# Local attention: queries' product and projection between the two score groups, values' product behind the second, input split three tiles ahead in two buffers

## The reference, cut to what matters

```python
h = shift_token(x)                         # right half of the channels moved down one token
q, k, v = split(h @ wqkv, 3)               # 256 -> 3 x 512, 8 heads of 64
q = l2norm(q) * q_scale;  k = l2norm(k) * k_scale
q, k = rotary_xpos(q, k)                   # x * cos + rotate_half(x) * sin, with a scale by position
# per window of 128 queries: keys and values are the window before and its own
sim  = einsum('bhwid,bhwjd->bhwij', q * 8, k)          # 128 x 256 per head
attn = softmax(where(mask, -max, sim))
o    = einsum('bhwij,bhwjd->bhwid', attn, v)
x = x + o @ wo
```

## Time and profile before

| what | value |
|---|---|
| median of 3 runs | 3078.51 us (3073.59 to 3085.33) |
| profiled execution, own time | 3081.87 us, span 3080.3 us, mean granted TensorE clock 0.935 |
| busy over the span | PE 2612.9 us (85%), PE weight loads 1544.9 (50%), DVE 2212.7 (72%), ACT 1491.3 (48%), POOL 542.4 (18%) |
| first layer's local attention | about 1483 to 2023 us |
| second layer's | about 2284 to 2824 us |
| largest groups of it | L1219 products 327.2 us PE (1152 matmuls), L1375 exponentials 284.1 us ACT, L1475 normalise 221.1 us DVE, L1540 powers 186.4 us POOL |
| means of smaller ones | L1459 scaling of the keys 692 ns DVE, L1382 `copy_probs` 595 ns ACT, L1365 `k_t` 612 ns, L1369 `q_t` 599 ns ACT |
| the chain of waits, as far as the page names it | PE 4%, DVE 2%, DMA 1%: it covers the last feed-forward phase only |

### The profile page before, as it was taken

How to read it: one execution, slowest core, us unless ns; L and a number is a source line. 1 busy time by engine, 2 the same in 40 slices (tenths; PEclk the granted TensorE clock), 3 DMA queues, 4 the chain that set the end, 5 groups by cost and what they waited for, 6 DMA issues and landing times. The chain is left out here.

```text
span 3080.3 us, 47691 instructions
## 1 busy us (share of the span) xinstructions
PE 2612.9 (85%) x14040; PEld 1544.9 (50%) x14040; DVE 2212.7 (72%) x4456; ACT 1491.3 (48%) x2777; POOL 542.4 (18%) x356
## 2 busy tenths in 40 slices
PE   4995899898898999884499999949969999995998
PEld 2442333333333333323366666628856666664777
DVE  5777788788887888866677777725547777774565
ACT  0320455555554555561366666624426666664343
POOL 0100000000100000015333333300013333331000
PEclk8996899999998999997799999979989999998999
DMA  2334244334344443416200000030001000000111
GB/s 87 120 108 105 68 127 126 98 97 120 100 113 114 119 115 97 99 60 234 70 9 8 8 9 9 4 111 21 20 15 48 8 7 9 9 7 31 55 57 42
DMA packets 122753, 204.93 MB, mean 67 GB/s; under 512 B 21728, under 2 KB 69920, under 8 KB 119216
## 3 DMA queue, kind: packets, MB, share of 16 engines
q1 hardware_dynamic: 108912, 163.96, 19.0%
q0 software_dynamic: 7808, 21.79, 2.4%
q10 hardware_dynamic: 5920, 17.75, 1.5%
HBM read 125.30 MB, written 54.26 MB: 58 GB/s over the span
## 5 line engine op out<-in xcount | busy, mean ns | idle before, releaser
L801 ACT ACTIVATE probs<-st_ps 128x1024 f32<-128x1024 f32 (+3 forms) x640 | 547.5, 895 | 525.0 <-PE st_ps L733 251.0
L749 PE MATMUL o_ps<-probs,vx 128*33 128x512 f32 (+3 forms) x2560 | 559.2, 560 | 0.0
L850 DVE SCALAR_TENSOR_TENSOR st_ps<-geo_rows,kp_t 128x512 f32<-128x512 f32 (+3 forms) x640 | 448.3, 716 | 77.9 <-ACT probs L801 73.7
L831 DVE TENSOR_REDUCE chunk_max<-a_ps 128x1 f32<-128x512 f32 (+3 forms) x640 | 367.0, 605 | 89.2 <-PE a_ps L721 50.1
L719 PE MATMUL a_ps<-k,q 96*128 96x512 f32 (+3 forms) x640 | 273.0, 476 | 80.9 <-DVE chunk_max L831 64.6
L1219 PE MATMUL local_in_ps<-w_local,local_ht 128*128 128x512 f32 x1152 | 327.2, 421 | 2.1 <-DVE local_ht L1426 2.1
L1375 ACT ACTIVATE local_probs<-local_s_ps,local_bias,local_inv 128x256 f32<-128x256 f32 x512 | 284.1, 571 | 14.2 <-DVE local_bias L1468 14.2
L1647 PE MATMUL ff_ag_ps<-ff_ht_parts,w 128*128 128x512 f32 (+1 forms) x1056 | 259.6, 404 | 32.2 <-DVE ff_gate L1756 24.0
L719 PEld LDWEIGHTS a_ps<-k,q 96*128 96x128 f32 x640 | 123.5, 203 | 278.0 <-issue 154.5
L733 PE MATMUL st_ps<-q,k 98*128 98x512 f32 (+3 forms) x640 | 225.8, 416 | 39.3 <-ACT probs L801 33.0
L1464 DVE TENSOR_REDUCE local_top<-local_s_ps 128x4 f32<-128x1024 f32 x128 | 156.7, 1224 | 135.9 <-PE local_s_ps L1261 135.9
(11 more groups left out here) (171 smaller groups left out, 3681.1 us busy)
## 6 DMA issues: line engine op xcount, KB each, us to landing
geo_rows<-geo SPq DMA_DIRECT2D x64, 512.0 KB, 7.2
q<-q_parts SPq DMA_DIRECT2D x48, 256.0 KB, 4.3
k<-k_parts SPq DMA_DIRECT2D x48, 256.0 KB, 6.3
piece_lo<-in_pieces POOLq DMA_DIRECT2D x15, 768.0 KB, 5.1
weight_parts<-piece_hi SPq DMA_DIRECT2D x15, 768.0 KB, 3.3
weight_parts<-piece_lo SPq DMA_DIRECT2D x15, 768.0 KB, 5.9
raw<-out_t SPq DMA_DIRECT2D x128, 64.0 KB
shares_in<-shares SPq DMA_DIRECT2D x64, 128.0 KB, 4.0
```

What stands on the lines that cost most here:

```text
L749: ins = pe.matmul(o_ps[kind * HALF:kind * HALF + VW, g % 2, off:GTOK], vx[s][:, j, :], probs[:, i % PSLOTS, kind, off:GTOK], start=j == 0, ...
L801: act.activation(probs[:, s % PSLOTS, :, off:GTOK], st_ps[:, s % 2, :, off:GTOK], ACT.Exp).then_inc(q["probs_ready"], 1)
L831: dve.reduce_max(chunk_max[:, it, c:c + 1], a_ps[:, s % 2, 0:n], AX.X).then_inc(q["a_used"], 1)
L850: ins = dve.scalar_tensor_tensor(out[:, off:GTOK], geo[:, 1, at], kp_t[:, j, ds(b, 1)].rearrange("p o -> p o"), geo[:, 0, at], ALU.add, AL ...
```

## The change

`ht` gets a second buffer. The input is transposed and split three tiles ahead instead of two (`make_later_input`), behind `weigh(t, 0)` instead of behind `weigh(t - 1, 3)`. The queries' product of t+2 goes between the two score groups, ahead of the projection; the values' product of t+1 goes behind scores B and the first two transposes of probabilities; the keys' product of t+2 goes behind the transposed queries. The projection writes bank 1 instead of bank 0. The squares wait for both rotations. On ScalarE the copy of the values goes behind the first two pairs of exponentials, the input's copy between the third and the fourth. On VectorE the residual goes behind `normalise(t, 1)`, the queries are rotated ahead of `normalise(t, 2)`, the low input stands between `normalise(t, 2)` and `(t, 3)`, and the keys are rotated last. GpSimd adds the queries ahead of the keys. The prologue and the written-out tiles (four at the end) follow.

```diff
@@ -1154,7 +1154,7 @@
-ht = sb("ht", [P, 2, CC, P], F32R)
+ht = sb("ht", [P, 2, 2, CC, P], F32R)
@@ -1182,13 +1182,13 @@
 def tiles(eng, body):
-    body(0, 0, 2)
-    body(1, 1, 2)
-    with eng.Fori(1, TILES // 2 - 1) as i:
+    body(0, 0, 3)
+    body(1, 1, 3)
+    with eng.Fori(1, TILES // 2 - 2) as i:
...
-            body(2 * i + p, p, 2, first=False)
-    body(LAST - 1, 0, 1)
-    body(LAST, 1, 0)
+            body(2 * i + p, p, 3, first=False)
+    for t in range(LAST - 3, LAST + 1):
+        body(t, t % 2, LAST - t)
@@ -1208,30 +1208,37 @@
     def _(pe):
         def make_input(u, p):
...
-            pe.wait_ge(q["sq_done"], at(u) + START)
...
-        def make_product(j, signal):
+        def make_later_input(u, p, after_output=True):
+            pe.wait_ge(q["sq_done"], at(u) - 1 + START)
+            if after_output:
+                pe.wait_ge(q["y_read"], at(u) - 3 + START)
+            make_input(u, p)
+        def make_product(j, p, signal):
...
-                last = pe.matmul(in_ps[:, j, :], ht[:, a, k, :], w[:, b, k, j * INNER:(j + 1) * INNER], start=i == 0, stop=i == len(steps) - 1)
+                last = pe.matmul(in_ps[:, j, :], ht[:, p, a, k, :], w[:, b, k, j * INNER:(j + 1) * INNER], start=i == 0, stop=i == len(steps) - 1)
...
-        def make_keys(u):
+        def make_keys(u, p, inputs=2):
+            pe.wait_ge(q["ht_low"], at(u) + inputs + START)
+            if inputs == 1:
+                pe.wait_ge(q["y_read"], at(u) - 2 + START)
+            make_product(1, p, q["k_ready"])
+        def make_queries(u, p):
...
-            make_product(1, q["k_ready"])
-        def make_queries(u, after_output=True):
...
-            if after_output:
-                pe.wait_ge(q["y_read"], at(u) - 2 + START)
-            make_product(0, q["q_ready"])
-        def make_values(u):
+            make_product(0, p, q["q_ready"])
+        def make_values(u, p):
...
-            make_product(2, q["v_ready"])
+            make_product(2, p, q["v_ready"])
         def transpose_rows(g, bank, signal):
@@ -1292,7 +1299,7 @@
-                last = pe.matmul(in_ps[:, 0, 0:C], o_t[:, x, :], wo[:, x, :], start=x == 0, stop=x == KIN - 1)
+                last = pe.matmul(in_ps[:, 1, 0:C], o_t[:, x, :], wo[:, x, :], start=x == 0, stop=x == KIN - 1)
...
         def tile(t, p, more, first=True):
@@ -1301,41 +1308,43 @@
             if not begins:
                 weigh(t - 1, 2)
                 weigh(t - 1, 3)
-            if more == 2:
-                make_input(t + 2, p)
+            if more >= 2:
+                make_queries(t + 2, p)
             if not begins:
                 project(t - 1, more)
-            if more:
-                make_values(t + 1)
             scores(t, p, 1)
             transpose_probs(t, 0, more)
             transpose_probs(t, 1, more)
-            if more == 2:
-                make_keys(t + 2)
+            if more:
+                make_values(t + 1, 1 - p)
             weigh(t, 0)
+            if more == 3:
+                make_later_input(t + 3, 1 - p, not begins)
             if more:
                 transpose_keys(t + 1)
-            if more == 2:
-                make_queries(t + 2, not begins)
             weigh(t, 1)
             if more:
                 transpose_queries(t + 1)
+            if more >= 2:
+                make_keys(t + 2, p, more - 1)
             transpose_probs(t, 2, more)
             transpose_probs(t, 3, more)
...
+        pe.wait_ge(q["ht_low"], at(1) + START)
+        make_input(1, 1)
...
-        make_keys(0)
-        make_queries(0, False)
-        make_values(0)
+        make_keys(0, 0)
+        make_queries(0, 0)
+        make_values(0, 0)
...
-        make_input(1, 1)
+        make_later_input(2, 0, False)
+        make_keys(1, 1)
+        make_queries(1, 1)
...
-        make_keys(1)
-        make_queries(1, False)
@@ -1343,15 +1352,16 @@
     @block.scalar
     def _(act):
-        def make_input(u):
+        def make_input(u, p, reused=True):
...
-            act.wait_ge(q["v_ready"], at(u) + START)
-            act.activation(ht[:, 0, :, :].rearrange("p k n -> p (k n)"), in_ps[:, 1, 0:CC * P], ACT.Copy).then_inc(q["ht_done"], 1)
+            if reused:
+                act.wait_ge(q["v_ready"], at(u) - 1 + START)
+            act.activation(ht[:, p, 0, :, :].rearrange("p k n -> p (k n)"), in_ps[:, 1, 0:CC * P], ACT.Copy).then_inc(q["ht_done"], 1)
         def make_squares(u):
...
+            act.wait_ge(q["rot_k"], at(u) + 1 + START)
@@ -1392,14 +1402,15 @@
                 make_squares(t + 1)
             if not begins:
                 copy_output(t - 1)
-                make_values(t, p)
             exponentials(t, p, 0)
             exponentials(t, p, 1)
-            if more == 2:
-                make_input(t + 2)
+            if not begins:
+                make_values(t, p)
             copy_probs(t, 0)
             exponentials(t, p, 2)
             copy_probs(t, 1)
+            if more == 3:
+                make_input(t + 3, 1 - p)
             exponentials(t, p, 3)
             if more:
                 make_keys(t + 1, 1 - p)
@@ -1407,11 +1418,12 @@
-        make_input(0)
+        make_input(0, 0, False)
+        make_input(1, 1, False)
...
-        make_input(1)
+        make_input(2, 0)
@@ -1421,10 +1433,10 @@
     @block.vector
     def _(dve):
-        def make_low_input(u):
+        def make_low_input(u, p):
...
-            dve.tensor_tensor(ht[:, 1, :, :].rearrange("p k n -> p (k n)"), in_ps[:, 1, 0:CC * P],
-                              ht[:, 0, :, :].rearrange("p k n -> p (k n)").bitcast(F32), ALU.subtract).then_inc(q["ht_low"], 1)
+            dve.tensor_tensor(ht[:, p, 1, :, :].rearrange("p k n -> p (k n)"), in_ps[:, 1, 0:CC * P],
+                              ht[:, p, 0, :, :].rearrange("p k n -> p (k n)").bitcast(F32), ALU.subtract).then_inc(q["ht_low"], 1)
         def make_rotated(u, g, ready, free, signal):
@@ -1478,7 +1490,7 @@
         def residual(t):
...
-            dve.tensor_tensor(S.x3[:, here, :], in_ps[:, 0:1, 0:C], S.x2[:, here, :], ALU.add).then_inc(q["y_read"], 1)
+            dve.tensor_tensor(S.x3[:, here, :], in_ps[:, 1:2, 0:C], S.x2[:, here, :], ALU.add).then_inc(q["y_read"], 1)
         def tile(t, p, more, first=True):
@@ -1486,26 +1498,27 @@
             if more:
                 make_norms(t + 1)
             normalise(t, 0)
+            normalise(t, 1)
             if not begins:
                 residual(t - 1)
-            normalise(t, 1)
-            if more == 2:
-                make_low_input(t + 2)
             maxima(t, p, 1)
             if more:
                 make_keys(t + 1, 1 - p)
-            if more == 2:
+            if more >= 2:
+                rotate_queries(t + 2)
+            normalise(t, 2)
+            if more == 3:
+                make_low_input(t + 3, 1 - p)
+            normalise(t, 3)
+            if more >= 2:
                 rotate_keys(t + 2)
-            normalise(t, 2)
-            normalise(t, 3)
-            if more == 2:
-                rotate_queries(t + 2)
...
-        make_low_input(0)
+        make_low_input(0, 0)
+        make_low_input(1, 1)
@@ -1514,9 +1527,9 @@
+        make_low_input(2, 0)
+        rotate_keys(1)
...
-        make_low_input(1)
-        rotate_keys(1)
@@ -1541,8 +1554,8 @@
         def tile(t, p):
             invert(t + 1, 1 - p)
+            add_queries(t + 2)
             add_keys(t + 2)
-            add_queries(t + 2)
         pool.dma_start(mask_even[:, :, :], io["mask_even"].rearrange("m p n -> p m n")).then_inc(S.masks_in, 16)
         pool.dma_start(mask_odd[:, :, :], io["mask_odd"].rearrange("m p n -> p m n")).then_inc(S.masks_in, 16)
```

## The result

The changed kernel takes 3030.07 us (median of 5 runs, 3028.51 to 3031.06) against 3078.51 us for the kernel before (3073.59 to 3085.33): ratio 0.984, 95% interval [0.9827, 0.9854]. The forecast was 3028 in 3014 to 3056. The profiled executions are 3029.94 us (span 3028.3) and 3081.87 us (span 3080.3).

What follows compares the result with a forecast made beforehand. Local attention is bound by PE's work plus two waits for copies. Gains 53.4 and 2.8 less losses 4.1 and 1.6 give 50.5 us, 3031.4 from the profiled 3081.87; 3028 from the runs' median, range 3014 to 3056.

Steps and rivals of the forecast that it cites:

- the stall: Steady tiles: 0.07 us a tile lost to the collision and two thin covers together, bounds 0 and 0.3.
- The two gaps: PE's waits for the copies of o_t and q_t in steady tiles close, gaining 0.92 us in the mean tile.
- The collision: GpSimd's addition of queries meets group 3's two multiplications, which end at 14.3; transposes 3 want them at 14.38.
- Masks B: Masks B come at 5.80 and can start after exponentials A at 5.65: cover 0.15 us, thinnest on the front half.
- The round trip: Input of t+3 from PE through ACT and DVE back to PE: low part 12.2, keys' product 12.34, cover 0.1.
- rival 1: Back-half covers fail together, low input or multiplications late by 0.3 to 0.6 us a tile: 3051 us, chance 0.19.
- Rival 2: No change: new waits take back 0.9 us a tile, with the collision on group 2: 3078 us, chance 0.07.
- Rival 3: Slower: the squares come too late, so the queries' product and all behind it wait: 3102 us, chance 0.08.
- Rival 4: The granted clock falls from 1.00; with shorter waits nothing speaks for it; no price or chance given.
- The start of a layer: Prologue splits two inputs before the first product: +0.8 us a layer, bounds -2 and +3.
- The ends: Last two tiles of a layer: same gaps go, about 0.9, and the values' copy, 0.5: -1.4 us a layer.
- the forecast's own range: Whole kernel, 3018 to 3040 us: stall 0 and gap 0.99 at one end, gap 0.77 at the other; chance 0.66.

Runs made afterwards that it cites:

- after: The kernel with the whole change and no further edit, against the kernel before: 3030.07 us, ratio 0.984.
- the two kernels under Together: Changed kernel with GpSimd's addition of queries behind normalise(t, 3) and next weights issued by SyncE: 3008.04 us; the same with the second input split later: 3003.58 us.

## Why the prediction was right

The mechanism was right in the steady tiles, the terms less so. Start of each step on PE from masks A, predicted and in the tile shown:

| step | predicted | measured |
|---|---|---|
| queries' product | 2.62 | 2.61 |
| projection | 4.19 | 4.12 |
| masks B | 5.80 | 5.85 |
| values' product | 8.25 | 8.28 |
| input | 10.41 | 10.45 |
| transposed keys | 10.85 | 10.72 |
| keys' product | 12.34 | 12.25 |
| transposes 2 | 13.91 | 13.74 |
| next masks A | 15.07, with the stall 15.14 | 15.12 |

- **The total was in part luck.** The steady tiles gained 54.7 us where 49.3 were forecast, 5.4 more; the starts lost 7.35 where 1.6 were forecast, 5.75 more. The two errors cancel. The 3028 against 3030.07 is closer than the terms that it is made of.
- **The two gaps.** They close, as forecast, shown by the waits of after and by the two experiments that open them again. The tile gained 0.92 and 0.96 us where 0.92 - 0.07 = 0.85 was predicted.
- **The collision.** Place and mechanism as predicted, size not: 0.36 us a tile instead of 0.07, outside its bounds (0 to 0.3). The multiplications were on time: in the tile ahead of the one shown (masks A 14.89 us before 1859.10) they start at 12.63 and end at 14.35, predicted 12.6 and 14.3. What failed is "transposes 3 want it at 14.38": PE starts transposes 2 at 13.72 there, and wants the other half 0.43 later, at 14.15. What offset it: I took 0.47 + 0.69 = 1.16 us for the last transposes, the 0.69 from a row that itself begins with a wait of 0.34. With nothing late they take 0.87, 0.29 less. Also the input cost 0.27 instead of 0.44 and the transposed queries 0.41 instead of 0.49, while the transposed keys took 0.53 instead of 0.41. Two errors of 0.3, of opposite sign, made the tile come out nearly right, which is luck too.
- **Masks B.** 1.73 us from the projection to them instead of 1.61, and no wait of theirs beyond single ones. Their cover was about 0.2 instead of 0.15, by what the values' copy cost once it was used up.
- **The round trip.** Cover about 0.3, not 0.1: in the tile ahead of the one shown the low part ends at 11.91 where the prediction had 12.2. That is why rival 1 had less for it than it seemed. Its other half, the multiplications late at transposes 3 by 0.3 to 0.6, did happen, at 0.36. That the time is not rival 1's 3051 is due to the cheaper transposes, and to this being half of it: the keys' product never waits in after.
- **Rival 2** didn't come: the addition starts at 1856.85, behind the transposed queries and beside group 3, not group 2. **Rival 3** didn't either: the squares of this tile start at 1859.90, 0.80 behind masks A, and are done at 1.82 (predicted 1.8), and the queries' product at 2.61 doesn't wait. **Rival 4**: the clock stays 1.00 in the steady tiles; it fell at the start of the layers instead.
- **The start of a layer** is the mis-sized term: +0.8 us predicted, +3.40 and +3.95 measured, beyond the bound of +3. The prediction named the second input and ScalarE's issues but gave the issues no price; it had the products of tile 1 moved ahead as a gain, and they had been what hid the issues. From masks A to B of tile 0, where the queries' product waits for the squares, it took 1.26 and 2.55 us more than before; from masks B to masks A of tile 1, partly at the lower clock (0.74 and 0.84 granted over this stretch, 1.00 before), 2.87 and 1.60 more (11.94 and 10.67 instead of 9.07); up to masks A, 0.73 and 0.20 less.
- **The ends** -1.45 and -1.48 for -1.4. The rest of the difference between the totals, -1.7, lies in code that wasn't changed.
- **Slips in the working.** The keys are scaled at 8.25 + 0.65 + 0.69 = 9.59, not "8.25 + 0.65 = about 9.55"; 9.55 is what the text goes on with, so nothing hangs on it. By its stated terms, from the median of the runs, the forecast's own range comes to about 3020 to 3037, not 3018 to 3040. And the waits were read from PE's rows alone, where the weight load's row of 16.0 us stood too.

What stays open: why the stretch ahead of local attention scatters by up to 14 us between kernels that have the same code there, which moves the totals of the small experiments; why the start of a layer scatters with the issues on ScalarE; and what the new place of the values' product is worth by itself, which no run isolates.

## What to carry to other kernels

Two waits in a row on PE didn't add here. And the distance from start to start beside a wait isn't a step's cost in a full pipe: the second half of the last transposes read 0.69 behind a wait and is 0.44 without (half of 0.87), the input 0.44 ahead of one and 0.27 without, while the projection read 1.61 behind a wait and 1.73 without. Take durations for a sum from rows with no wait in or beside them. A wait listed for a weight load is a place to look, not a price: the 16.0 us listed before were worth nothing, the 9.5 listed after went with 10.7 us of the first layer's tiles. When a change moves work, ask again for each pair of VectorE and GpSimd instructions who waits for it: here the same 64 us of VectorE time was worth nothing in one order and 21 us in the other, for one added wait on GpSimd. Check the start of a layer as a stage of its own: a queue of DMA issues on a compute engine is a wait for whatever that engine does next, and work moved away from beside it lays it bare.

## What the runs showed of the hardware

- A collision of VectorE and GpSimd costs in either order of start: the multiplications took 1.72 us though GpSimd's addition started 0.01 us behind them in the record (0.62 alone), as they had taken 1.67 when it started 0.03 ahead. I had expected the one that starts first to go free. Which one really went first can't be read at that distance. GpSimd's addition lost nothing in either (1.28 and 1.29 us, 1.28 alone).
- PE busy at 208.88 of 210 us was no sign of a full engine: 0.36 us in 14.95 was still to be had, and with it gone PE is busy 209.38 of the same 210. The Trainium skill (Perfetto Trace Analysis, section Identifying the Most-Contended Engine) says that matmul busy time is not a good measure of how close a kernel is to roofline; these two traces agree.
- Six DMA issues on ScalarE took 3.2 us, 0.39 to 0.71 each.
- The granted clock at the start of a layer was 0.51 for 6 us behind a wait of 2.66 us. Behind a wait of 2.26 us it was 1.00 in both layers of the kernel with the weights issued by SP and in the first layer of the two kernels under Together, and 0.83 or 0.84 in their second. Where the queries' product waited for the squares (2.55 to 3.77 us) the clock was below 1.00 in every layer from masks A to B of tile 0, but not always behind masks B: with the collision alone removed, layer 2 had 0.79 before them and 1.00 from there to the next masks A. What decides is open; in after the price from masks B to masks A of tile 1 was 2.9 and 1.6 us.
